# A transformer layer on one core: batch 0 gets loads and an order of its own, segment rows come by a one-hot matmul, weights are centred by a matmul, and half step 0 runs over the keys of one half and then of the other

## The reference, cut to what matters

```python
h = segm_table[segment] + pos[None] + token_table[x]          # (8, 1024, 192)
n = layernorm(h)
q, k, v = (n @ qkv_weight.T).reshape(B, N, 3, H, D) ...
q = layernorm(q) * D ** -0.5                                   # over the 16 of each head
k = layernorm(k)
out = softmax(q @ k.T) @ v
h = h + out @ proj_weight.T
xq = round(clip(layernorm(h) / mean(alpha_a1), -8, 7))         # and so for w1, w2, gelu's result
h = h + ffn(xq)
```

## Time and profile before

| | us |
|---|---|
| median of 3 runs | 1113.6 (1111.63 to 1113.84) |
| the profiled execution | 1112.17 |
| its span, first to last instruction | 1110.2 |
| TensorE busy in it | 972.4 (88%) |
| ScalarE busy | 868.3 (78%) |
| VectorE busy | 814.5 (73%) |
| GpSimd busy | 432.5 (39%) |
| granted TensorE clock, mean share of full speed | 0.971 |

### The profile page before, as it was taken

How to read it: one execution, slowest core, us unless ns; L and a number is a source line. 1 busy time by engine, 2 the same in 40 slices (tenths; PEclk the granted TensorE clock), 3 DMA queues, 4 the chain that set the end, 5 groups by cost and what they waited for, 6 DMA issues and landing times.

```text
span 1110.2 us, 19437 instructions
## 1 busy us (share of the span) xinstructions
PE 972.4 (88%) x7535; PEld 380.3 (34%) x7535; DVE 814.5 (73%) x2289; ACT 868.3 (78%) x936; POOL 432.5 (39%) x354
## 2 busy tenths in 40 slices
PE   1246999999999999999999999999999999989883
PEld 1132333333434342433434343424334343413131
DVE  6486556978878786969788787869697787815265
ACT  0244788889798979889898979788897989798961
POOL 3766161263534443453635344443535312201011
PEclk9985999999999999999999999999999999999995
DMA  8421010020301112020302031020303000000000
GB/s 206 75 26 22 9 22 9 1 44 1 66 7 30 16 40 33 1 44 1 72 2 35 9 57 16 19 26 1 44 1 44 1 16 1 16 1 15 1 15 14
DMA packets 26681, 29.37 MB, mean 26 GB/s; under 512 B 5056, under 2 KB 23168, under 8 KB 26592
## 3 DMA queue, kind: packets, MB, share of 16 engines
q0 software_dynamic: 18432, 12.59, 9.8%
q1 hardware_dynamic: 7184, 14.86, 4.2%
q10 hardware_dynamic: 976, 0.70, 0.3%
HBM read 21.85 MB, written 6.29 MB: 25 GB/s over the span
## 4 chain that ended last, share of the span: by engine, by line
PE 42%; ACT 33%; DVE 15%; POOL 4%; issue 4%; DMA 2%; POOLq 0%; SPq 0%; DVEq 0%; ACTq 0%
ACT probs L535 25%; PE ps_o L890 15%; PE ps_s L873 9%; PE ps_j L918 4%; ACT gelu L529 4%; PE ps_j L970 3%; POOL stack L462 3%; PE ps_j L931 3%; PE ps_j L926 2%; PE ps_j L937 2%; ACT L529 2%; PE ps_j L956 2%; ACT L535 2%; PE ps_j L941 2%; DVE stack L655 1%
## 5 line engine op out<-in xcount | busy, mean ns | idle before, releaser
L535 ACT ACTIVATE probs<-ps_s 128x1024 f32<-128x1024 f32 x768 | 736.2, 1024 | 125.4 <-PE ps_s L873 118.4
L890 PE MATMUL ps_o<-probs,v_sb 128*32 128x512 f32 x3072 | 396.1, 607 | 0.0
L873 PE MATMUL ps_s<-qT,kT 64*128 64x512 f16 x1536 | 266.8, 386 | 37.7 <-ACT probs L535 27.0
L462 POOL TENSOR_TENSOR stack<-sq,stack 128x384 f16<-128x384 f32 x128 | 123.7, 987 | 148.8 <-DVE stack L655 148.8
L873 PEld LDWEIGHTS ps_s<-qT,kT 64*128 64x128 f16 x1536 | 62.5, 93 | 305.8 <-ACT probs L535 270.9
L471 POOL TENSOR_TENSOR y_sb<-y_sb,b_row 128x768 f32<-128x768 f32 x16 | 29.1, 1817 | 277.5 <-DVE y_sb L729 277.5
L409 POOL DMA_INDIRECT h_all<-in_L_tok_token_table,idx x64 | 103.0, 1610 | 73.9 <-DMA h_all<-in_L_tok_segm_table,idx 59.3
L890 PEld LDWEIGHTS ps_o<-probs,v_sb 128*32 128x32 f32 x3072 | 69.4, 109 | 124.3 <-issue 116.1
L409 POOL DMA_INDIRECT h_all<-in_L_tok_segm_table,idx x64 | 99.8, 1560 | 26.7 <-issue 15.5
L453 POOL TENSOR_TENSOR sq<-qk 128x384 f32<-128x384 f32 x56 | 46.3, 827 | 146.2 <-DVE qk L692 146.2
L529 ACT ACTIVATE gelu<-ps_j,b_sb,s_sb 128x512 f32<-128x512 f32 x96 | 70.1, 775 | 26.3 <-PE ps_j L956 25.3
(11 more groups left out here) (122 smaller groups left out, 1057.4 us busy)
## 6 DMA issues: line engine op xcount, KB each, us to landing
h_all<-in_positions SPq DMA_DIRECT2D x8, 768.0 KB
out<-h_all SPq DMA_DIRECT2D x16, 384.0 KB
qT<-in_L_ffn_w SPq DMA_DIRECT2D x2, 576.0 KB, 8.1
h_all<-in_L_tok_segm_table,idx POOLq DMA_INDIRECT x64
h_all<-in_L_tok_token_table,idx POOLq DMA_INDIRECT x64
probs<-in_L_attn_qkv_weight SPq DMA_DIRECT2D x2, 432.0 KB, 4.9
probs<-in_L_ffn_alpha_a ACTq DMA_DIRECT2D x1, 384.0 KB, 5.0
probs<-in_L_attn_proj_weight SPq DMA_DIRECT2D x1, 144.0 KB, 5.7
```

Source lines behind the costliest of these rows:

```text
L462: last = nc.gpsimd.tensor_tensor(low, src, high, ALU.subtract)
L535: nc.scalar.activation(probs[:, u % PROBS, 2 * pair:2 * pair + 2], ps_s[:, 2 * pair:2 * pair + 2], ACT.Exp, scale=SCORE_SCALE).then_inc(ex ...
L873: last = mm(ps_s[:, j], kT[rows, par, head // 2, m * P:(m + 1) * P], qT[rows, par, head // 2, nh * NQ:(nh + 1) * NQ], start=True, stop=True)
L890: last = mm(ps_o[32 * j:32 * j + 2 * D, :], v_sb[:, par, m, (GH * group + j) * VE:(GH * group + j) * VE + 2 * D], probs[:, u % PROBS, j], ...
```

## The change

It touches the opening and half step 0.

- Loads: batch 0's tokens first, its positions in two halves, weights between them, no waits; batch 0's segment indices and the segment table go by ScalarE's queue. The other batches' indices and the feed-forward's data come after. The feed-forward's raw weights lie in another buffer.
- Tokens of half 0 are gathered plainly into `y_sb`, and VectorE adds them tile by tile (`first_rows`). Half 1's tokens are gathered onto the positions. Batch 0's segment rows are a product of a one-hot matrix (3 rows) with the table, added by VectorE from PSUM.
- GpSimd gathers segments of halves 2 and 3 before half 0's low parts, tokens of half 2 after them, tokens of half 3 after half 1's low parts.
- q and k weights are transposed and centred in one product with `cen` (identity less 1/16 within each block of 16). ScalarE writes the scaled high parts from PSUM, VectorE the low parts. ScalarE makes an exponential of one column at the very start.
- Half 0 is normalised tile by tile, and VectorE makes the low part of its keys. ScalarE squares q and k of halves 0 and 1 from PSUM ahead of the copy.
- Half step 0 has an order of its own (`START_PLAN`, words with a half behind the dot, lower case a to d are ScalarE's copies) with six passes: three head groups over half 0's keys, then three over half 1's. The second three are added to `o_sb` (`head_outputs`). Its scores wait for four tiles, from unit 12 for eight.
- W moves to half step 1, w and the constants (z) to the end of half step 0.

```diff
 PLAN = """
 h h o
-Y0 Y1 Y2 F0 Y3 w0 F1
+Y0 Y1 Y2 F0 Y3 F1
...
+START_PLAN = """
+P0.0 R0.0 v0.0 N0.0 A0.0 A1.0 A2.0 a0.0 a1.0 P0.1 B0.0 a2.0 B1.0 b0.0 B2.0 b1.0 r0.0 A3.0 a3.0 b2.0 B3.0 r1.0 b3.0 C0.0 c0.0 R0.1 r2.0 r3.0 C1.0 S0.0 C2.0 h n0.0 c1.0 D0.0 d0.0 n1.0 E0.0 n2.0 c2.0 D1.0 h E1.0 n3.0 N0.1 d1.0 D2.0 C3.0 d2.0 c3.0 E2.0 D3.0 A0.1 d3.0 a0.1 A1.1 A2.1 a1.1 a2.1 A3.1 B0.1 a3.1 B1.1 b0.1 r0.1 b1.1 r1.1 B2.1 E3.0 b2.1 B3.1 r2.1 b3.1 C0.1 r3.1
+S0.1 n0.1 C1.1 C2.1
+h
+h
+h n1.1 D0.1 E0.1 n2.1
+h o D1.1 E1.1
+n3.1 h
+P0.2 R0.2 h
+D2.1 C3.1
+N0.2 D3.1 h
+h E2.1 A0.2
+A1.2 A2.2 B0.2 A3.2 B1.2 r0.2 o B2.2 r1.2 E3.1
+B3.2 h
+h h r2.2
+r3.2 h S0.2 n0.2
+o n1.2 C0.2 C1.2
+h
+D0.2 h
+D1.2 E0.2 h n2.2
+h o E1.2 C2.2
+h h n3.2
+h h z0.2 o
+D2.2 C3.2 E2.2
+w0.2 h
+w1.2 h D3.2 E3.2
...
-FIRST_PLAN = """
-P0 R0 N0 A0 A1 A2 A3 v0 P0' R0' N0' B0 B1 r0 B2 r1 B3 r2 C0 C1 r3 C2 C3 S0
-A0' A1' A2' A3' B0' B1' n0 n1 r0' r1' D0 E0 n2 B2' D1 E1 n3 B3' r2' C0' D2 E2 r3' D3 E3 S0'
-n0' n1' C1' C2' C3' D0' E0' n2' D1' E1' n3' D2' E2' D3' E3'
-"""
-FIRST_WORK = [(w[0], int(w[1]), -1 if w[2:] else -2) for w in FIRST_PLAN.split()]
-
-
-
-FIRST_GATHERED = 3
+FIRST_GATHERED = 4
...
+def unit_work(s0):
+    return UNIT_WORK if s0 else STEP0_WORK
+
+
+def passes(s0):
+
+    return HG if s0 else 2 * HG
+
+
+def copies_to(s0):
+
+    return HG * s0 + (HG if s0 else 0)
+
+
+def unit_tile(s0, u):
+
+    per = UNITS // passes(s0)
+    p, m = divmod(u, per)
+    return p % HG, p // HG * per + m
...
-    return s0 == 0 if kind == "W" else 0 <= job_half(kind, s0) < HALVES
+    return s0 == 1 if kind == "W" else 0 <= job_half(kind, s0) < HALVES
...
+            sp.dma_start(idx_in[:, 0, 0:1], x_v[:, 0:1]).then_inc(tok_loaded, 16)
+            sp.dma_start(wq_nat[:, :, 0:C], w_v).then_inc(w_loaded, 16)
+            sp.dma_start(h_all[:, 0:half], pos_v[:, 0:half]).then_inc(first_pos[0], 16)
+            sp.dma_start(wq_nat[:, :, C:2 * C], w_v).then_inc(w_twice, 16)
+            sp.dma_start(h_all[:, half:2 * half], pos_v[:, half:2 * half]).then_inc(first_pos[1], 16)
+            sp.dma_start(wp_nat, w_proj.rearrange("(r p) c -> p r c", p=KC)).then_inc(wp_loaded, 16)
+            sp.dma_start(idx_in[:, 1, 1:B], seg_v[:, 1:B]).then_inc(idx_loaded, 16)
+            sp.dma_start(idx_in[:, 0, 1:B], x_v[:, 1:B]).then_inc(idx_loaded, 16)
+            load_pos(1)
...
-            add_segments(0)
-            pool.wait_ge(idx_ready, 2)
-            add_tokens(0)
-            add_segments(1)
-            add_tokens(1)
-            add_segments(2)
-            add_tokens(2)
+            for t in range(TH):
+                nc.gpsimd.indirect_dma_start(
+                    out=y_sb[:, t], out_offset=None, in_=tok_table,
+                    in_offset=bass.IndirectOffsetOnAxis(ap=idx[:, 0, t:t + 1], axis=0)).then_inc(tok_first[t], 16)
+            pool.wait_ge(rows_added, 2)
+            gather(tok_table, 0, 1, tok_added[1])
...
+                    for high, low, src in parts_ if s0 > -2 else parts_[:1]:
...
-            for s in (-2, -1):
-                split_low(s, s)
+            pool.wait_ge(idx_ready, 3)
+            add_segments(2)
+            add_segments(3)
+            split_low(-2, -2)
+            add_tokens(2)
+            split_low(-1, -1)
+            add_tokens(3)
...
+            act.wait_ge(scale_ready, 1)
+            for n, (dst, src) in enumerate(weight_halves(wh)):
+                act.wait_ge(w_mm, 1 if n < 4 else 2)
+                nc.scalar.activation(dst, src, ACT.Copy, scale=w_scale[:]).then_inc(high_weights, 1)
...
+            def first_rows():
+
+                for t in range(TH):
+                    dve.wait_ge(tok_first[t], 16)
+                    last = tt(h_tile(0, t), h_tile(0, t), y_sb[:, t], ALU.add)
+                link(last)
...
+                if s0 == -2:
+                    for t in range(TH):
+                        link(ts(hn[:, t], h_tile(half, t), mv[:, 0, t, 0:1], rn[:, 0, t:t + 1], ALU.subtract, ALU.mult))
+                        link(nc.vector.tensor_copy(parts[:, t, 0:C], hn[:, t]))
+                        tt(parts[:, t, C:2 * C], hn[:, t], parts[:, t, 0:C], ALU.subtract).then_inc(hn_first, 1)
+                    return
...
+                if s0 == -2:
+
+                    dve.wait_ge(high_ready, t + 1)
+                    tt(low, src, high, ALU.subtract).then_inc(low_k_ready, 1)
...
+            def head_outputs(s0, s, p):
+
+                dve.wait_ge(heads_mm, UNITS * s + UNITS // passes(s0) * (p + 1))
+                group = o_sb[:, p % HG]
+                if p < HG:
+                    ins = nc.vector.tensor_copy(group, ps_o[:])
+                else:
+
+                    dve.wait_ge(heads_out, p - HG + 1)
+                    ins = tt(group, ps_o[:], group, ALU.add)
+                ins.then_inc(heads_out, 1)
...
+                    last = ts(hot[:, :, k], idx_f[:, 1, 0], float(k), None, ALU.is_equal)
+                last.then_inc(hot_ready, 1)
...
+                    dve.wait_ge(first_pos[n], 16)
+                    dve.wait_ge(rows_mm, n + 1)
+                    for i in range(2):
+                        hv = h_all[:, (2 * n + i) * 2 * C:(2 * n + i + 1) * 2 * C]
+                        last = tt(hv, ps_s[:, 2 * n + i, 0:2 * C], hv, ALU.add)
+                    last.then_inc(rows_added, 1)
...
+                dve.wait_ge(scale_ready, 1)
+                for n, ((dst, src), (high, _)) in enumerate(zip(weight_halves(wl), weight_halves(wh))):
+                    if n in (0, 1, 3):
+                        dve.wait_ge(high_weights, n + 1)
+                        last = stt(out=dst, in0=src, scalar=w_scale[:], in1=high, op0=ALU.mult, op1=ALU.subtract)
+                last.then_inc(weights_ready, 1)
...
+                        last = mm(ps_s[:, at // 2, at % 2 * C:(at % 2 + 1) * C], hotT[:, at * P:(at + 1) * P], seg_rows,
+                                  start=True, stop=True)
...
+                        last = mm(ps_j[:, m, r * KC:(r + 1) * KC], wq_nat[:, r, m * P:(m + 1) * P], cen[:], start=True, stop=True)
...
-                    pe.wait_ge(job_out["D"], (s + 2) * TH)
-                    pe.wait_ge(job_out["E"], (s + 2) * TH)
+                    pe.wait_ge(job_out["D"], (s + (2 if s0 else 1)) * TH)
+                    pe.wait_ge(job_out["E"], (s + (2 if s0 else 1)) * TH)
+                if s0 == 0 and u == UNITS // 2:
+                    pe.wait_ge(job_out["D"], 2 * TH)
+                    pe.wait_ge(job_out["E"], 2 * TH)
```

More of the change, by code:

```diff
@@ L105, with words @@
 JOB_KINDS = "ABCDEFGHIWXY"
-UNIT_WORK = [[] for _ in range(UNITS)]
-TAKEN = {"h": 0, "o": 0, "g": 0}
-for unit_work, unit_line in zip(UNIT_WORK, PLAN.strip("\n").split("\n")):
-    for word in unit_line.split():
-        if word in TAKEN:
-            unit_work.append((word, TAKEN[word]))
-            TAKEN[word] += 1
-        else:
-            unit_work.append((word[0], int(word[1])))
-JOBS = [w for unit in UNIT_WORK for w in unit if w[0] in JOB_KINDS]
-GELU_UNIT = next(u for u, unit in enumerate(UNIT_WORK) if ("g", 0) in unit)
+def words(plan, first_copy):
+    taken, units = {"h": 0, "o": first_copy, "g": 0}, []
+    for line in plan.strip("\n").split("\n"):
+        units.append([])
+        for word in line.split():
+            if word in taken:
+                units[-1].append((word, taken[word], 0))
+                taken[word] += 1
+            else:
+                units[-1].append((word[0], int(word[1]), int(word[3:]) if word[2:] else None))
+    return units
@@ new lines @@
+S0.1 n0.1 C1.1 C2.1
[22 more added lines that the diff above has]
+w1.2 h D3.2 E3.2
+"""
+FIRST_WORK, *STEP0_WORK = [[(k, t, half if half is None or k in "ho" else half - 2) for k, t, half in line]
+                           for line in words(START_PLAN, 1)]
@@ L171, in job_before @@
         if bank_of(other, s) == bank_of(job, s0):
-            return other, s0 - s
+            return other, s
     return None
-def copied_by_act(kind, part, s0):
-    return s0 < 0 and kind in "ABCD"
 def layer(nc, x_tok, x_seg, tok_table, seg_table, w_qkv, w_proj, w1, b1, aw1, aa1, w2, b2, aw2, aa2,
@@ new lines, in _ @@
+            nc.scalar.activation(wpT[:], ps_s[0:KC, 1, 0:2 * C].rearrange("p (k c) -> p k c", k=2),
+                                 ACT.Copy).then_inc(proj_ready, 1)
+            def copy_out(s0, s, kind, t):
+                half = job_half(kind, s)
+                act.wait_ge(job_mm[kind], nth(half, t, TH))
+                if kind == "B":
+                    square(s0, s, t)
+                scale = w_back[:] if kind in "BC" else 1.0
+                for dst, src in copies(s0, s, kind, t):
@@ L685, in job_result @@
                 ps = bank(job, s0)
-                for part, (dst, src) in enumerate(copies(s0, s, kind, t)):
-                    if copied_by_act(kind, part, s0):
+                for dst, src in copies(s0, s, kind, t):
+                    if (kind, t, s0) in ACT_COPIES:
                         continue
```

346 lines of the change are left out of this document (208 added, 138 removed).

## The result

The changed kernel takes 1077.8 us, the median of 4 runs (1076.59 to 1078.42), against 1113.0 for the one before: a ratio of 0.968, with a 95% interval of 0.967 to 0.970. The forecast was 1083 with 1070 to 1096. The sign and the range held, and so did the main of the mechanism: latencies in a row set the opening, the split of the keys is its largest part, and VectorE's list ends last up to unit 12. Two steps did not hold: TensorE's work in the opening was priced at nothing beside VectorE and is what VectorE waits for, and VectorE is 1.0 us behind at the start of half step 1, not 5.0. The gain is 35.3 us where 28.8 was forecast, so 6.5 us of it came from terms with a wrong size. The traced execution of the changed kernel took 1076.6 us, the shortest of its four, so differences read between traces can be off by about 1 us from those between medians.

The account below looks back on a forecast made before the run. Latencies in a row bound the opening, TensorE and ScalarE the steady part. Terms 125.1 + 60.1 + 2.4 = 187.6 against 216.4 gave 28.8 us less than 1112.2, so 1083, range 1070 to 1096.

Parts of the forecast that it names:

- TensorE's work in the opening: Opening: centring products, one-hot transposes and row products lie beside VectorE's work, priced at nothing, 0 to 3 us if uncovered.
- Early loads and rows: Start of the opening: first gather at 5.7, tokens landed at 17.8, VectorE free for them at 18.0.
- From tokens to the first exponential: Rest of the opening: from 18.0 through first split at 40.1 to first exponential at 62.0, a gain of 35.9 us.
- The 2 us that the forecast set on four tiles: Half 0's key splits: if VectorE and GpSimd exclude each other, four tiles take some 2 us longer, 1085.
- GpSimd's cover: Opening: twelve gathers end at 37.7, the first low part is wanted at 41.3, so 3.6 us to spare.
- the rival in which they come late: Opening: GpSimd's twelve gathers slow to 2.21 us, end 4.3 us after they are wanted, 1088; chance 14%.
- VectorE's list up to unit 12: First part of half step 0: VectorE's list of 32.5 us bounds it, from 61.0 to 93.5, unit 12 at 95.0.
- The end of half step 0: VectorE's list after the last B copy ends at 127.9, so half step 1 counts as started at 125.1, not 120.1.
- W: Half step 1: six TensorE groups and six VectorE copies moved there lengthen it by 2.4 us.
- ScalarE alone: Half step 0: VectorE's list keeps ahead and 48 exponentials set the step at 50.3 us, total 1071; chance 13%.
- The split of keys: Opening: rival that it brings nothing, as unit 0 still waits for half 1; first exponential at 78, total 1095; chance 7%.
- The rival of the low clock: Half steps 0 and 1: stalls keep TensorE at 1.2 GHz, + 95 us, or + 44 for half step 0 alone (1127); chance 2%.

Follow-up runs that it names:

- Experiment 3: Changed kernel with the 12 centring products of the q and k weights replaced by plain transposes, so the head mean stays in: 1075.4 us.
- experiment 2: Changed kernel with half 0's token additions and norm statistics put into VectorE's wait for the largest weight: 1075.6 us.
- experiment 1: Changed kernel with the constants (z, 3.9 us of VectorE work) moved from the end of half step 0 to ahead of unit 12: 1084.0 us.
- experiment 7: Changed kernel without the quantising of the feed-forward's weights on VectorE in half step 0: 1078.0 us.
- experiment 6: Changed kernel without the products that make the feed-forward's transposed weights in half step 1, zeros in their place: 1076.1 us.
- experiment 5: Changed kernel with half step 0 as one pass over all keys again, half 1's splits back in the opening: 1094.2 us.
- experiments 8: Changed kernel with early half 0 token additions and statistics, and the largest weight's transpose ahead of the centring products on TensorE: 1074.8 us.
- 9: Changed kernel with batch 0's segment rows by accumulating gathers from HBM again instead of one-hot products: 1090.7 us.
- 10: As experiments 8, with loads of the feed-forward's weights and later positions held until half 1's tokens have landed; against the changed kernel: 1073.7 us.

## Why the prediction was right, and where it was off

**Early loads and rows.** Forecast: first gather 5.7, each 1.85, VectorE's token additions at 18.0. Measured: 3.56, 1.25, and 19.94. The last plain gather was through at 8.48 (12.9 forecast) and took 6.4 us to land (4.9), so the tokens were there 3 us earlier than thought, and it bought nothing. The forecast priced TensorE's opening work beside VectorE at nothing with 0 to 3 on top, by the 22 transposes of the earlier trace rows. That was the term that decided: row products 5.48 us and centring 5.84 us stand in TensorE's list ahead of the transpose that VectorE waits for. Old and new transposes and products are not "of like size": 12 centring products took 5.84 us where 12 transposes take 2.6. Experiment 3 takes this off TensorE and experiment 2 fills VectorE's wait with other work; the first exponential comes 2.6 and 2.0 us earlier. The bound of 3 us was right, the value taken was the wrong end.

**From tokens to the first exponential.** First A transpose 28.13 (26.3 forecast), first split 41.11 (40.1), first exponential 61.17 (62.0). That the first exponential came within 0.8 of its forecast is partly luck: the delay of 1.8 was made good in three places, 13.0 us from the first A to the first split (13.8 forecast), 9.1 for half 0's splits (9.8), 11.0 from there to the first exponential (12.1). The 2 us that the forecast set on four tiles if VectorE and GpSimd take turns did not come: they do take turns (the four scalings take 0.56, 1.26, 0.76 and 0.76 us), and that costs 1.1, inside the 9.1. GpSimd's cover was 7.3, not 3.6, since its twelve gathers began at 12.80 and not at 15.5 and took 1.54 to 1.68 us each; the rival in which they come late did not happen, though two later gathers did take 1.77 and 2.03 us beside VectorE's work.

**VectorE's list up to unit 12.** Its kind was right: experiment 1 shows that it ends last there. Its size was not: 28 us from the first exponential to E3.1's copy, where 32.5 was summed, so unit 12 came at 89.87 and not 95.0. Norm and root took 4.2 as forecast, the way to the first split 4.1 (4.3), N0.2 2.7 (2.9). Two terms failed. Splits, C, D and E copies and a head copy were 9.4 + 4.5 + 0.7 = 14.6; they took 12.0. A and B copies were 1.4 + 5.1 = 6.5; they took 5.1, with the square sums and one more head copy in between. Both terms were distances between rows of the old trace, the splits' 9.4 and the B cadence of 1.70, and those held waits for other engines. In the 5.1 us of the B cadence VectorE is idle 2.3 us (1.08, 0.62 and 0.62). In the splits' 9.4 it is idle 1.8 us:

```profile
88.71 0.56 DVE L694 COPY kT<-ps_j 128x768 f16<-128x768 f16 x1 [1.40 <-PE ps_j L931]
...
90.79 0.56 DVE L694 COPY kT<-ps_j 128x768 f16<-128x768 f16 x1 [0.39 <-PE ps_j L931]
```

The forecast took this 1.8 off for half 0's splits and left it in for half 1's and half 2's. In the new list other words fill these waits (it is idle 0.19 and 0.41 us there), and the forecast added the words to the waits.

**The end of half step 0.** The forecast had VectorE 5.0 us behind when half step 1 starts, by 33.4 us of list after the last B copy. Measured 1.0, by experiment 7. The failed step is the same: terms read as distances that hold waits. The head copy was to end at 127.9 and ended at 119.98: 5.5 us of that came with the last B copy (89.03 for 94.5), 2.4 from the list after it (31.0 us for 33.4). The half step itself began 3.9 earlier, so the backlog shrank by 4. This is the largest wrong term. Of the signs that the forecast named, the single stall ahead of unit 12, a first gather at 5 to 6 us and VectorE busy over 90% of half step 0 (49.2 of 55.0 us) did not come.

**W.** Forecast 2.4, measured 2.8 by experiment 6. The rest of half step 1's 3.3 is most likely the late head copy: without the quantising (experiment 7) the half step is 0.6 shorter, 116.97 to 179.80.

**The rivals.** ScalarE alone did not set half step 0 (50.3 us forecast for that, 55.0 measured), but the result lies between that rival and the forecast, since the list was shorter. The split of keys was the largest part: without it 1094.2, where the rival had 1095. That these agree is partly luck, for the rival had the first exponential at 78 and a half step of 58.4, and experiment 5 has 81.2 and 52.5. The rival of the low clock did not happen in the changed kernel (1.00 in half steps 0 to 13, 0.94 in half step 14, where little but attention is left), but experiment 1 shows it in small, in half step 0.

**The sum.** Against the forecast: the first exponential 0.8 earlier, half step 0 3.1 shorter (55.0 for 58.1), half step 1 with its backlog 4.1 shorter (63.4 for 67.5), and 1.4 lost in the rest, together 6.6. The 0.8 is within the scatter of the opening.

## What to carry to other kernels

A list's cost is what its instructions take back to back. The distance from one to the next in an old trace is that only after the idle time between them is taken out: a new order fills those waits. When a wait is removed from an in-order list, look at the next word that waits for data of a later stage. Here each gain ahead of half 1's statistics was lost or kept by that one word's place (experiments 8, 9, 10). And where buffers are given out by a word's place in a plan that all steps share, a word moved for one step changes the rotation in all of them.

## What was not expected of the hardware

- A float32 product of 96 columns took 0.49 us in a run of them (5.84 for 12), and a transpose of the same tile 0.22 (2.6 for 12).
- An indirect gather that only writes took 0.95 us of GpSimd, one that accumulates 1.55.
- In experiment 1 TensorE was idle 2.28 and 2.65 us within 5 us, the granted clock of that stretch was 0.70, and 3.9 us of VectorE work cost 6.2. In the changed kernel TensorE is busy 10.96 of 12.00 us where its stalls lie (80 to 92), and the clock stays at 1.00.
